# Decoder layer on one core: the start regrouped around one projection weight at a time, and a new order for all engines

## The reference

```python
def reference(x, ctx_1024, mask, head_dim_mask, w_q, w_k, w_v, w_o, W, b, w_gate, w_up, w_down):
    x = x + attn(_layernorm(x))       # q, k, v = x w_q, x w_k, x w_v; softmax(q k^T / sqrt(128)) v * mask; w_o
    x = x + xattn(_layernorm(x))      # relu(x W^T + b) relu(ctx W^T + b)^T, masked softmax, times ctx
    x = x + ffn(_layernorm(x))        # silu(gate) * up, then down; weights ternary, activations 8 bits
    return x
```

## Time and profile before

| | |
|---|---|
| median of 3 runs | 376.03 us (375.55 to 376.86) |
| profiled execution, its own time | 375.11 us |
| its span in the trace | 373.3 us |
| PE busy | 362.1 us, 97% of the span |
| ACT busy | 318.2 us, 85% |
| DVE busy | 314.7 us, 84% |
| POOL busy | 293.2 us, 79% |

### The profile page before, as it was taken

How to read it: one execution, slowest core, us unless ns; L and a number is a source line. 1 busy time by engine, 2 the same in 40 slices (tenths; PEclk the granted TensorE clock), 3 DMA queues, 4 the chain that set the end, 5 groups by cost and what they waited for, 6 DMA issues and landing times.

```text
span 373.3 us, 7341 instructions
## 1 busy us (share of the span) xinstructions
PE 362.1 (97%) x2108; PEld 278.7 (75%) x2108; DVE 314.7 (84%) x914; ACT 318.2 (85%) x590; POOL 293.2 (79%) x421
## 2 busy tenths in 40 slices
...
GB/s 277 266 222 257 6 169 29 20 118 91 73 28 101 56 128 139 35 126 35 128 94 152 70 99 59 195 14 62 124 57 108 27 60 42 72 29 100 56 116 112
DMA packets 47591, 36.92 MB, mean 99 GB/s; under 512 B 39232, under 2 KB 40896, under 8 KB 47168
## 3 DMA queue, kind: packets, MB, share of 16 engines
...
## 4 chain that ended last, share of the span: by engine, by line
PE 77%; ACT 6%; DVE 4%; DMA 4%; issue 4%; POOL 3%; SPq 1%; ACTq 0%; DVEq 0%; POOLq 0%
PE b_bank L1054 9%; PE b_bank L1056 9%; PE b_bank L1055 9%; PE d_bank L1285 6%; PE g_bank L1269 5%; PE a_bank L1054 5%; PE a_bank L1056 5%; PE a_bank L1055 5%; PE u_bank L1269 5%; PE b_bank L1197 3%; PE a_bank L1117 3%; DMA x_all<-in_x 2%; PE b_bank L1168 2%; DMA c_half<-c_half 2%; PE e_bank L1055 1%
## 5 line engine op out<-in xcount | busy, mean ns | idle before, releaser
L685 POOL TENSOR_TENSOR c_work<-c_work 128x512 f32<-128x512 f32 x48 | 61.6, 1291 | 8.1 <-DVE c_work L1519 5.3
L944 ACT ACTIVATE c_work<-g_bank,c_tanh_scale 128x512 f32<-128x512 f32 x52 | 35.9, 691 | 7.3 <-PE g_bank L1269 3.8
L732 POOL TENSOR_SCALAR c_work<-c_work,h_q 128x1024 f32<-128x1024 f32 x31 | 34.9, 1124 | 8.5 <-DVE h_q L1553 8.3
L1054 PE MATMUL b_bank<-ctx_hi,b_pT_hi 128*128 128x256 f32 x128 | 39.3, 307 | 0.0
L1519 DVE SCALAR_TENSOR_TENSOR c_work<-c_work,g_bank 128x512 f32<-128x512 f32 x50 | 33.8, 675 | 4.5 <-ACT c_work L944 4.5
L1055 PE MATMUL b_bank<-ctx_lo,b_pT_hi 128*128 128x256 f32 x128 | 36.1, 282 | 0.0
L1056 PE MATMUL b_bank<-ctx_hi,b_pT_lo 128*128 128x256 f32 x128 | 36.1, 282 | 0.0
L1285 PE MATMUL d_bank<-downT,c_half 128*128 128x256 bf16 x256 | 33.3, 273 | 2.0 <-ACT a_xT_raw L971 0.7
L1546 DVE TENSOR_REDUCE h_max<-c_work 128x1 f32<-128x1024 f32 x28 | 33.9, 1211 | 1.2 <-POOL c_work L685 1.0
L1269 PE MATMUL g_bank<-gateT,xqT 128*128 128x512 bf16 x112 | 33.6, 382 | 0.2 <-ACT c_work L932 0.2
L1269 PE MATMUL u_bank<-upT,xqT 128*128 128x512 bf16 x112 | 33.6, 381 | 0.0
...
## 6 DMA issues: line engine op xcount, KB each, us to landing
...
```

Of the source, the lines that this page charges most:

```text
L685: pool.tensor_tensor(h[:, t % 2, half * HALF:(half + 1) * HALF], th[:, j % 2, :], up[:, j % 2, :], ALU.mult).then_inc(hs, 1)
L732: pool.tensor_scalar(h[:, t % 2, :], h[:, t % 2, :], h_q[:, t:t + 1], ROUND if n < LAST else ROUND_F16, ALU.mult, ALU.add).then_inc(h_roun ...
L944: act.activation(th[:, j % 2, :], gu_bank("g", j, n), ACT.Silu if (n, j) in SILU else ACT.Tanh, scale=c_tanh_scale[:, j // 2:j // 2 + 1]). ...
L1054: pe.matmul(dst, l_hi, r_hi, start=first, stop=False)
```

## The change

- The column sum becomes three steps W.sumQ, W.sumK, W.sumV, each 128 columns wide in a bank of its own, and the centring three steps W.centreQ, W.centreK, W.centreV. Q/0 waits for the first alone, K/0 for two, V/0 for all three. W.qkv on ACT waits for all three.
- x^T of sequence 0 is loaded in two DMAs (W.t0, W.t1) right behind the weights, ahead of x, W and ctx^T. Q/0 waits for each half before the matmul that reads it.
- E.YP0/0 moves from ahead of Q/0 to behind K/0 on PE, and W.r from behind V/0 to ahead of it.
- All five order lists are new.

```diff
-A_FRONT = """YP0/0 Q/0 K/0 V/0 S0/0 S1/0 VT/0 S2/0 S3/0 P0/0 YP1/0 P1/0 Q/1 P2/0 K/1 P3/0 V/1 H/0 YP0/1 VT/1 S0/1
+A_FRONT = """Q/0 K/0 V/0 S0/0 S1/0 VT/0 YP0/0 S2/0 S3/0 P0/0 YP1/0 P1/0 Q/1 P2/0 K/1 P3/0 V/1 H/0 YP0/1 VT/1 S0/1
...
-    W.qkv/0 W.W/0 W.c/0 W.t/0 W.x0/0 W.x1/0 S.x/1 S.xT/1 F.gate/0 W.o/0 S.ctxT/1 S.mask/0 S.mask/1 S.rw/1 F.up/0
+    W.qkv/0 W.t0/0 W.t1/0 W.x0/0 W.x1/0 W.W/0 W.c/0 S.mask/0 S.ctxT/1 S.xT/1 W.o/0 S.x/1 F.gate/0 S.mask/1
...
+        sum_bank = [b1_bank, d_bank, u_bank]
...
-        xT0_loaded = sem("xT0_loaded")
+        xT0_loaded = [sem("xT0_front_loaded"), sem("xT0_back_loaded")]
...
-                elif name == "t":
-                    sp.dma_start(xT_first[:, :, :], x_t[:, 0]).then_inc(xT0_loaded, 16)
+                elif name[0] == "t":
+                    c = int(name[1])
+                    sp.dma_start(xT_first[:, c, :], x_t[:, 0, c, :]).then_inc(xT0_loaded[c], 16)
...
                 elif name == "qkv":
-                    act.wait_ge(qkv_centred, 1)
+                    act.wait_ge(qkv_centred, 3)
...
             def project_first(dst, step):
                 w = "QKV".index(step)
-                if step == "Q":
-                    pe.wait_ge(qkv_centred, 1)
-                if step == "Q":
-                    pe.wait_ge(xT0_loaded, 16)
+                pe.wait_ge(qkv_centred, w + 1)
                 for c in range(DC):
+                    if step == "Q":
+                        pe.wait_ge(xT0_loaded[c], 16)
...
-                if name == "colsum":
+                if name[:3] == "sum":
                     pe.wait_ge(qkvo_loaded, 16)
+                    w = "QKV".index(name[3])
                     for c in range(DC):
-                        mm = pe.matmul(b1_bank[:, 0:3 * DH], ones[:, :], wqkv_raw[:, c, :, :].rearrange("p w d -> p (w d)"),
-                                       start=c == 0, stop=c == DC - 1)
+                        mm = pe.matmul(sum_bank[w][:, 0:DH], ones[:, :], wqkv_raw[:, c, w, :], start=c == 0, stop=c == DC - 1)
...
                 elif name == "r":
                     pe.wait_ge(r0_spread, 1)
-                    pe.wait_ge(qkv_centred, 1)
+                    pe.wait_ge(qkv_centred, 3)
...
-            def centre_qkv():
-                dve.wait_ge(qkv_sums, 1)
+            def centre(w):
+                dve.wait_ge(qkv_sums, w + 1)
                 for c in range(DC):
-                    raw = wqkv_raw[:, c, :, :].rearrange("p w d -> p (w d)")
-                    last = dve.scalar_tensor_tensor(raw, b1_bank[:, 0:3 * DH], -1.0 / D, raw, ALU.mult, ALU.add)
+                    raw = wqkv_raw[:, c, w, :]
+                    last = dve.scalar_tensor_tensor(raw, sum_bank[w][:, 0:DH], -1.0 / D, raw, ALU.mult, ALU.add)
```

More of the change, by code:

```diff
@@ L84 @@
 PE_ORDER = """
[L85 to L114, removed]
@@ new lines @@
+    W.sumQ/0 W.sumK/0 W.sumV/0 A.Q/0 A.K/0 E.YP0/0 W.r/0 A.V/0 A.S0/0 A.S1/0 A.VT/0 A.S2/0 E.YP1/0 A.S3/0 A.P0/0
+    A.P1/0 A.Q/1 A.P2/0 A.K/1 A.P3/0 A.V/1 E.YP0/1 A.H/0 A.VT/1 A.S0/1 A.S1/1 A.Y0/0 E.YP1/1 A.S2/1 A.P0/1
+    A.Y1/0 A.S3/1 F.total/0 A.P1/1 A.P2/1 A.P3/1 E.YP0/2 A.H/1 B.XT0/0 B.XT1/0 E.YP1/2 A.Y0/1 B.XP0/0 B.XP1/0
+    A.Y1/1 A.Q/2 A.K/2 B.S0/0 B.S1/0 A.V/2 B.P0/0 B.S2/0 A.VT/2 B.P1/0 A.S0/2 B.O0/0 B.S3/0 B.P2/0 A.S1/2 B.O1/0
+    B.P3/0 A.P0/2 A.S2/2 B.O2/0 A.P1/2 A.S3/2 B.O3/0 B.XT0/1 A.P2/2 A.P3/2 E.YP0/3 B.XT1/1 A.H/2 B.XP0/1 B.XP1/1
```

251 lines of the change are left out of this document (139 added, 112 removed).

## The result

| | before | changed |
|---|---|---|
| median | 375.96 us (375.55 to 376.86, 4 runs) | 373.08 us (372.73 to 373.73, 4 runs) |
| ratio | | 0.992 (0.990 to 0.994) |
| span of the profiled execution | 373.3 us | 371.0 us |

The change made the kernel 2.9 us faster; forecast were 375.9 us and a range of 374.2 to 377.6. The same pair, measured again beside the experiments, gave 0.9957 (0.994 to 0.9974), which is 1.6 us. Both intervals exclude 1; my estimate of the size is about 2 us, between them.

The account below looks back on a forecast made before the run. PE was taken as full from 60 to 280 us, the start as bound by PE up to first scores, then ACT to 47.49. Start -0.1 and tail 0.0 gave -0.1 us: 375.9 us, range 374.2 to 377.6.

Parts of the forecast that it names:

- PE is full from 60 to 280 us, so nothing is won there: Middle of the kernel: PE has no idle time, so a new order gains nothing; a wait appearing there was priced at zero.
- Sums 2.1 us: Start, on PE: the three column sums take 2.1 us, sumV ending at 6.0, between 5.2 and 6.9.
- Second half of x at 8.5 us: Start, loads: this half lands at 8.5 us, in proportion to the KB ahead in the queue; ends 7.9 and 10.35.
- `vT` 1.76 us: Start, on DVE: `vT` keeps its earlier length of 1.76 us, ending at 13.75.
- W.split 12.0, W.r 13.8: Start: W.split on DVE ends at 12.0 us, W.r on PE starts at 13.8 against 15.63, after `vT`.
- Sums, x^T and the move of YP0/0 at nothing, hidden by the wait for `vT`: Start, on PE: these edits cost nothing thanks to slack before W.r; up to 0.9 us without it.
- The 1.8 us won on W.r are spent on V/0: Start, on PE: V/0 now lies behind W.r, so first scores start at 16.5 against 16.60, 0.1 us gained.
- ACT's net -0.1: ACT up to 47.49 us: common work starts 0.71 us later, 0.81 us of waits go; bounds -0.7 and +0.7.
- Tail 0.0: End of the kernel: C.DN1/5's wait goes, -0.67; ACT's longer list before B.XP0/7, +0.7; bounds -0.7 and +1.0.
- a sign against me: ACT waiting again between W.r and 47 us, named beforehand as showing the prediction wrong.
- (2): Rival, faster, 26%: second half of x lands at 7.9, W.r at 13.2, start -0.7 and tail -0.7, 374.6 us.
- (3): Rival, slower, 25%: fixed time from issue to landing, x no earlier; at 10.35 the start is 1.75 us worse, 377.8 us.

Follow-up runs that it names:

- the rest alone: Kernel before up to about 50 us, behind that the new order lists; 375.22 us, ratio 1.0003 to the kernel before.
- x^T whole: Changed kernel with x^T of sequence 0 loaded in one DMA of 512 KB, Q/0 waiting for all of it; 373.44 us, ratio 0.994.
- the start only: Changed kernel up to about 50 us, behind that the old order lists; 373.11 us, ratio 0.994 to the kernel before.
- x last: Changed kernel with W and ctx^T loaded ahead of x^T and x again; 375.44 us, ratio 1.0003 to the kernel before.

## Why the prediction was wrong

Two steps failed, both on the way to W.r: the landing of the second half of x (8.5 us forecast, 7.1 measured) and the length of `vT` (1.76 us forecast, 0.68 measured). With them fell the wait for `vT` that was to hide all else. Step by step:

- *PE is full from 60 to 280 us, so nothing is won there.* Right as to the gain: the rest alone gives 1.0003. But something can be lost there, and was priced at zero: the new list brings 0.5 to 1.5 us of waiting ahead of C.DN0/4, and waits of 0.5 to 0.8 us for the transposed `xqT` stand near 140 us in some traces. That the rest comes out at nothing is partly luck, since the tail's 0.4 us covers most of this.
- *Sums 2.1 us.* 2.69 in the first trace, 1.8 in the one with x^T whole, 2.1 with the start only; the bounds held.
- *Second half of x at 8.5 us.* About 7.1. This is one of the two steps that failed. I spread the time between the landing of ctx^T (7.88) and the last landing (10.35) by bytes, and all nine traces with the new queue lie below that (7.0 to 7.8). Why is not shown. Part of it may be that landings differ between executions: ctx^T, now the last of the same 2176 KB, landed at 8.9 (3.5 + 5.4), where I had 10.35.
- *`vT` 1.76 us.* 0.68. The other step that failed; beside a POOL instruction the changed kernel loses 1.0 us. The 1.76 of the earlier trace rows held a wait for POOL's `a_xT_lo`, and the order that I showed moves `a_xT_hi`, which that POOL step needs, behind W.r's copy: POOL cannot be in the way any more.
- *W.split 12.0, W.r 13.8.* 10.9 and 11.81. From x 1.4 us, from W.centreV 0.1 (0.46 us in place of 0.6; by the Trainium skill, "VectorE: DVE Perf Modes", the section on the trn2 errata, the estimate was 0.52), from `vT` 1.1; against them stood 0.5 that I had left out, since ACT copies Q/0 before W.qkv. `vT` was ready at 11.49, so W.r waited for PE alone.
- *Sums, x^T and the move of YP0/0 at nothing, hidden by the wait for `vT`.* With that wait gone the cover was gone. One sum instead of three costs 0.85 us, close to the 0.9 that I had as the price without cover; the halves of x^T are worth nothing that can be seen; YP0/0 could not have stayed. That PE came to YP0/0 at 10.09, near the forecast 10.35, is luck: PE was late from the sums, and ctx^T had long landed.
- *The 1.8 us won on W.r are spent on V/0.* True for PE (first scores at 14.10 with W.r behind V/0, at 14.38 and 14.60 ahead of it) but not for the kernel: W.r's place is worth 1.1 us, through ACT.
- *ACT's net -0.1.* The ledger took W.r's copy at 14.97; it came at 12.87. With that, its own working gives -2.2, and measured are -2.3 (45.15 against 47.49). The sum was built rightly on a start that was wrong, though ACT did wait again between W.r and 45 us (0.45, 0.23 and 0.26 us for its longest waits), which I had named as a sign against me.
- *Tail 0.0.* Both effects are in the trace with the forecast signs (DN1/5's 0.67 us gone, XP0/7 waits 0.55), and from 310 us to the end the lead goes from 1.9 to 2.3 us, within its bounds.
- *The rivals.* (2) named the right direction and the right cause, an early x, but stopped at -0.7 us at the start, since it kept 1.76 us for `vT` and took 7.9 for x. (3), a fixed time to landing, is refuted: the halves landed in 4.2 and 4.5 us instead of 7.2 and 7.3, and in 6.7 and 6.9 us with x last. The Trainium skill's 2.0 us fixed per DMA ("DMA: Bandwidth & Descriptors", anatomy of one DMA) is a fit for DMAs issued from GpSimd; here SP issues them, and I set that time ahead of x as if the fixed parts queued up. The traces don't show that: with one DMA for x^T in place of two the second half of x landed at 7.2 us instead of 7.1.
